# Layer 0's node table made beside the fetch of the edge rows, with ScalarE normalising

## The chip, the cores and the metric

One NeuronCore of a Trainium2 chip runs the whole program in one launch. The engines are PE (TensorE, matmuls and transposes), DVE (VectorE), ACT (ScalarE), POOL (GpSimd) and SP (SyncE, which only issues DMAs here). The metric is the device time of one execution in microseconds (us); lower is better.

## The reference, cut to what matters

Four layers of a graph network run over 6250 nodes of 128 features and 100,000 edges, sorted by destination. Each layer normalises the features, and layer 0 then gathers them over the edges:

```python
h = jnp.maximum(_layernorm(x, axis=-1), 0.0)
x = x + _L0_gnn_ref(h, edge_index, edge_weight, W, gamma, beta, 6250, 6250)

rows, cols = (A_indices[0], A_indices[1])        # src, dst
gathered = x[cols] * A_values[:, None]
h = jax.ops.segment_sum(gathered, rows, num_segments=m)
h = jnp.einsum('md,od->mo', h, W)
h = (h - mean) * jax.lax.rsqrt(var + BN_EPS) * gamma + beta
return jax.nn.relu(h)
```

So layer 0 takes its rows by `dst` (in sorted order) and adds them up by `src` (in random order). Layers 1 to 3 gather by `src` and add up by `dst`; layer 3 uses the small weights `Wl1` and `Wl2`.

## The kernel before

**Nodes and items.** The nodes lie in SBUF as `X`, 50 blocks of 128 rows (NBT is 50, the last block is empty, NB is 49). The edges are cut into rows of 128. Since the edges are sorted by destination, a row of edges touches one block of nodes or a few; each pair of an edge row and a block is an *item*, and there are 832 of them (ITEMS), in turns of 16 (RING). META is 896, seven chunks (CHUNKS) of 128 items.

**Prologue (lines 404 to 423, 591 to 713, 766 to 792, 1065 to 1083, 1270 to 1395).** SP loads `dst`, `X` and then the weights, in this order, on one queue. ACT issues the DMAs that copy `src`, `dst` and the edge weights to `e_meta` (three rows of 128 for an edge row, semaphore `small_copied`), and the block number of each edge to `blk_f` and `blk_i` (`blocks_out`), which only a sorting branch for unsorted inputs reads; that branch is not taken here. DVE and ACT count the edges below each block (lines 1282 and 1078), DVE turns the counts into the plan of the items (lines 1293 to 1327, `blocks_ready`): for each item its edge row and its block. POOL waits for `blocks_out` and `small_copied`, then fetches the edge rows of all items with seven indirect gathers (L703, semaphore `meta_rows`), fetches the rows once more in plain order (L708, L710), and sets two of the four sum buffers in DRAM to zero; the other two it did at the start (L636). PE transposes the three weights of layers 0 and 1 (L775), and DVE copies them out (L1362) and splits the biases into three bfloat16 parts (L1363 to L1368, `bias_split`). When the edge rows are in, DVE converts them to floats (L1377 to L1383), and 28 transposes on PE with 28 copies on DVE (L784, L1389) make `src_it`, `rel_it`, `w_it` and `m_row`, in which a column is an item. Last, 14 transposes and four copies make `blk_row` and `row_row` (L787 to L789, L1393, L1394), the lists from which the engines load the block and the edge row of an item into registers. A barrier (`barrier`, lines 263 to 267: all five engines drain and wait for each other) ends the prologue.

**Layer 0's table (`node_tables(0)`).** SP first stores `m_row` to DRAM (L543). DVE takes the statistics of the 50 blocks (L1400) and makes from them the reciprocal of the deviation and the product of that and minus the mean (L1423 to L1432), with a square root on ACT between (L1088). Then 13 batches of four blocks (the last of two) go through a pipeline: DVE multiplies and adds in two passes (L1406, L1410), PE transposes four blocks (L804), ACT copies them out with Relu (L1095), PE multiplies them with W0 (L820), ACT copies the product into the table `Tz` in SBUF (L1105). POOL and SP wait at the barrier that ends the table. `big`, the large region of SBUF, holds both the fetched edge rows (from 0 on) and `Tz` (from 0 on), so one follows the other.

**Layer 0's edges (`edges0`).** First DVE makes `to_spare` (L1521, L1522). Then all engines run through the items in steps; step n works on item n in its first stage and on earlier ones in the later stages. For an item: DVE builds a one-hot matrix (L1528), PE transposes it (L880), ACT copies it out (L1137), PE multiplies it with one block of `Tz` (L888), ACT scales by the edge weight (L1144). SP has meanwhile spread the 128 source ids of the item over all partitions (L448); DVE compares them with each other (L1536), PE adds up edges of the same source (L896), and six steps after the item's first stage DVE copies the result to `z_out` (L1544). L1550 and L1555 find repeated sources, whose rows are sent to a spare place. Every eighth step DVE makes eight columns of indices at once (L1568, semaphore `idx_ready`), and POOL adds each item's 128 rows into one of four buffers in DRAM with an indirect DMA (L727), in the order of the items; it waits for `idx_ready` at each eighth item, for `out_ready`, and for the previous scatter into the same buffer. SP also copies pieces of the edge attributes in this stage (L456), three DMAs for each turn of 16 items.

**After it.** `batch_norm` adds the four buffers and normalises; then come layers 1 to 3. At the start of each of these POOL sets the accumulator in `big` to zero (L747) while DVE begins `node_tables`. In layer 1 DVE first scales `Wl1` and `Wl2` (L1419 to L1421).

The order of the work is written out by hand; there is no planner. The main wait of the edge stage on POOL reads:

```python
if k % GROUP == 0:
    held(pool, ph["idx_ready"], uses[0])
held(pool, ph["out_ready"], i + 1)
held(pool, scattered[k % COPIES], uses[1])
```

## Time and profile before

| | |
|---|---|
| median of 3 runs | 5306.88 us (5306.61 to 5311.04) |
| the profiled execution | 5307.79 us |
| its span, first to last instruction | 5306.1 us |
| busy: PE, DVE, ACT, POOL | 4042.5, 3448.4, 1884.1, 3745.5 us |
| mean granted TensorE clock | 0.775 of full |

All times in the profile are from the start of the span. A busy share of the whole span says little here, since the stages have different limits; the stages are read from the windows and the timeline. "Idle before" is the time in which an engine did nothing ahead of an instruction, and the name behind "<-" is the releaser, the event that ended it. "issue" means that nothing in the profile was waited for. A name with q behind it (SPq, DVEq) is an engine's sequencer.

### The profile page before, as it was taken

What the parts mean: (1) busy time and instruction counts of PE and PEld (TensorE: products, weight loads), DVE (VectorE), ACT (ScalarE), POOL (GpSimd) and SP (SyncE); (2) the same over time, 40 slices, a digit from 0 to 9 for tenths busy, and PEclk for the clock granted to TensorE, in tenths of its full rate; (3) what the DMA queues carried; (4) which work ended last, traced back from release to release, by engine and by line L of the source; (5) the groups of instructions that cost most, each with busy time, mean ns of one, the idle gap of its engine ahead of it and who ended that gap; (6) DMA issues with size and microseconds to landing.
All of it is one profiled execution on the core that took longest, in us unless ns stands there. A gap on an engine that the chain in (4) does not pass through costs nothing. (4 is left out here: it accounts for less than half of the span.)

```text
span 5306.1 us, 109574 instructions
## 1 busy us (share of the span) xinstructions
PE 4042.5 (76%) x21313; PEld 3091.3 (58%) x21314; DVE 3448.4 (65%) x11120; ACT 1884.1 (36%) x5384; POOL 3745.5 (71%) x3284
## 2 busy tenths in 40 slices
PE   2888888888884466666666899998998678787787
PEld 2666666665663344444445677777776555565556
DVE  6655655656553633333335788888887688888886
ACT  3322222222221122222222433443343555555553
POOL 1888888888885377777773477777776277777772
PEclk8655555555555678888888999999999888888889
DMA  5656666665666266666663566666665233332332
GB/s 174 103 90 92 90 92 90 92 90 89 93 89 124 65 180 177 180 180 180 179 180 101 158 198 198 196 201 194 198 198 164 79 57 56 56 56 56 56 56 58
DMA packets 937554, 658.88 MB, mean 124 GB/s; under 512 B 402828, under 2 KB 878955, under 8 KB 934290
## 3 DMA queue, kind: packets, MB, share of 16 engines
q0 software_dynamic: 212176, 281.46, 26.3%
q1 hardware_dynamic: 722294, 372.22, 26.2%
q10 hardware_dynamic: 2812, 2.00, 0.2%
q8 instruction: 118, 1.93, 0.2%
q14 instruction: 154, 1.26, 0.1%
HBM read 462.32 MB, written 224.57 MB: 129 GB/s over the span
## 5 line engine op out<-in xcount | busy, mean ns | idle before, releaser
L727 POOL DMA_INDIRECT sums<-work,idx x832 | 1285.5, 1545 | 323.3 <-issue 173.9
L1497 DVE TENSOR_TENSOR x_and_big<-psum,x_and_big 128x129 f32 (+2 forms) x2496 | 830.3, 333 | 701.0 <-PE psum L843 484.8
L759 POOL DMA_INDIRECT G<-table,src_it x832 | 863.3, 1038 | 324.2 <-issue 252.9
L759 POOL DMA_INDIRECT G<-table,work x782 | 770.0, 985 | 269.5 <-issue 235.3
L759 POOL DMA_INDIRECT x_and_big<-table,work x782 | 762.0, 974 | 272.2 <-issue 236.2
L896 PE MATMUL psum<-work 128*128 128x128 f32 x1664 | 622.7, 476 | 194.5 <-DVE work L1544 167.2
L1144 ACT ACTIVATE work<-psum,work 128x128 f32<-128x128 f32 x832 | 306.1, 368 | 1067.0 <-PE psum L888 1065.2
L896 PEld LDWEIGHTS psum<-work 128*128 128x128 f32 x1664 | 408.2, 304 | 383.8 <-DVE work L1544 379.6
L990 PE MATMUL psum<-x_and_big,oh 128*128 x1664 | 513.3, 463 | 127.2 <-DVE x_and_big L1684 114.6
L843 PE MATMUL psum<-x_and_big,oh 128*128 x1664 | 322.4, 353 | 369.7 <-DMA x_and_big<-table,work 277.8
L888 PE MATMUL psum<-x_and_big,work 128*128 x1664 | 585.0, 454 | 0.0
L843 PEld LDWEIGHTS psum<-x_and_big,oh 128*128 128x128 f32 x1664 | 273.0, 248 | 462.8 <-issue 462.8
L1536 DVE TENSOR_SCALAR work<-G,src_it 128x128 f32<-128x128 int32 x832 | 270.8, 325 | 387.4 <-PE psum L896 380.4
L990 PEld LDWEIGHTS psum<-x_and_big,oh 128*128 128x128 f32 x1664 | 364.0, 229 | 215.1 <-issue 159.3
L880 PE MATMUL psum<-ident,oh 128*128 128x128 f32 x832 | 362.9, 436 | 88.3 <-issue 30.4
L888 PEld LDWEIGHTS psum<-x_and_big,work 128*128 128x128 f32 x1664 | 409.0, 305 | 34.3 <-issue 9.1
L1167 ACT ACTIVATE work<-work 128x512 f32<-128x512 f32 x208 | 131.2, 631 | 658.7 <-DVE work L1598 658.7
L1544 DVE COPY work<-psum 128x128 f32<-128x128 f32 x832 | 242.8, 292 | 184.5 <-DMA sums<-work,idx 181.1
L925 PE MATMUL psum<-x_and_big 128*128 x2496 | 345.1, 282 | 19.3 <-DVE work L1598 19.3
L1618 DVE TENSOR_TENSOR work<-work,G 128x1024 f32<-128x1024 f32 x208 | 254.7, 1224 | 142.4 <-DMA G<-table,src_it 141.2
L1484 DVE TENSOR_TENSOR oh<-iota,rel_it 128x512 f32<-128x512 f32 x416 | 285.2, 686 | 86.4 <-issue 82.1
L1194 ACT ACTIVATE x_and_big<-work 128x64 f32<-128x64 f32 x784 | 208.6, 336 | 365.8 <-DVE work L1663 365.8
(240 smaller groups left out, 7290.2 us busy)
## 6 DMA issues: line engine op xcount, KB each, us to landing
work<-e_pre SPq DMA_DIRECT2D x832, 128.0 KB
e_pre<-work SPq DMA_DIRECT2D x196, 512.0 KB
G<-e_meta SPq DMA_DIRECT2D x832, 64.0 KB, 3.1
work<-e_a SPq DMA_DIRECT2D x195, 128.0 KB
e_a<-in_edge_attr_dram SPq DMA_DIRECT2D x51, 488.0 KB
sums<-work,idx POOLq DMA_INDIRECT x832
G<-table,src_it POOLq DMA_INDIRECT x832
sums<-x_and_big POOLq DMA_DIRECT2D x4, 3264.0 KB
```

The lines of the kernel that those rows point to most:

```text
L727: pool.indirect_dma_start(sums[k % COPIES], bass.IndirectOffsetOnAxis(ap=idx[:, k:k + 1], axis=0), z_out[:, k, :], None, compute_op=ALU.ad ...
L759: pool.indirect_dma_start(to, None, tab, bass.IndirectOffsetOnAxis(ap=of[:, n:n + 1], axis=0)).then_inc(quad_in[n // 4 % AHEAD], 16)
L843: mm = t.matmul(bank[2 * o + j // 2][:, j % 2 * wid:(j % 2 + 1) * wid], oh[:, (k - 1) % 4 * 4 + j, :], at(G1, slot), start=True, stop=True)
L880: t.transpose(bank[s % 2][:, 0:P], oh[:, s, :], ident[:]).then_inc(ph["t_done"], 1)
L888: t.matmul(bank[2 + s % 2][:, 0:P], ohT[:, s % 4, :], at(Tz, b), start=True, stop=True).then_inc(ph["row_done"], 1)
L896: t.matmul(bank[4 + s % 2][:, 0:P], same[:, s % 4, :], scaled[:, s % 4, :], start=True, stop=True).then_inc(ph["sum_done"], 1)
L925: mm = t.matmul(pre_bank(half)[:, j % 2 * 256:j % 2 * 256 + 256], ohT2[:, (k - 1) % 2, j, :], Qp[:, bass.ds(b, 1), piece * 256:(piece + 1) ...
L990: mm = t.matmul(bank[4 + k % 2 * 2 + j // 2][:, j % 2 * 256:j % 2 * 256 + 256], oh[:, k % 4 * 4 + j, :], at(msg3, slot), start=True, stop= ...
L1144: a.activation(scaled[:, s % 4, :], bank[2 + s % 2][:, 0:P], ACT.Copy, scale=w_it[:, bass.ds(n - 4, 1)]).then_inc(ph["w_done"], 1)
L1484: v.tensor_tensor(oh[:, k % 4 * 4:k % 4 * 4 + 4, :], iota[:].unsqueeze(1).broadcast_to([P, 4, P]), rel_it[:, bass.ds(q * 4, 4)].unsqueeze( ...
L1497: v.tensor_tensor(to, ps, to, ALU.add).then_inc(EDGE[layer]["acc_done"], 1)
L1536: v.tensor_scalar(same[:, s % 4, :], src_b[:, s, :], src_it[:, bass.ds(n - 1, 1)], None, ALU.is_equal).then_inc(ph["same_ready"], 1)
```

## The change

What it does, by engine:

- **Memory.** The fetched edge rows and the setup region move behind the first NBT * 128 columns of `big`, so that `Tz` can be written while they are in use.
- **POOL.** Its gathers no longer wait for `blocks_out`. The barrier ahead of layer 0's table and the one behind it become one. The first turn of 16 scatters is written out; it waits for `idx_ready` at items 0, 2, 4, 6 and 8, the loop at each eighth as before.
- **PE.** The 14 transposes for `blk_row` and `row_row` come first, then the weights. Layer 0's table is made in the prologue: in step i PE transposes batch i, multiplies batch i - 1 and transposes two of the 28 pieces of the edge rows.
- **ACT.** After the counts it takes the square root, then normalises each block with one `Relu` with scale and bias from columns, four for a batch, and copies the transposed batch out. The product is now copied into `Tz` by DVE.
- **DVE.** Statistics and `layer_norm` come right behind the plan, with the copies of `blk_row` and `row_row` between the variance and the reciprocal; then the weights and biases, the conversions in another order with a signal after each, and a loop with two copies of edge pieces and one of the table in each step; then `to_spare`, then the barrier.
- **DVE, edge stage.** At steps 3, 5, 7 and 9 two columns of indices are made; from step 17 on eight at once, as before.
- **SP.** `X` gets a semaphore of its own. The first 16 loads of source ids and the store of `m_row` come ahead of the barrier, the attribute copies behind it.
- **Wl1 and Wl2** are scaled in `batch_norm`, behind the last sum and ahead of the wait for the mean, and no more in layer 1.

```diff
-        m_row = big[:, 8 * META:9 * META].bitcast(I32)
+        MB = NBT * 128
+        m_row = big[:, MB + 8 * META:MB + 9 * META].bitcast(I32)
...
-        setup_at = [16000]
+        setup_at = [MB + 9 * META + (NBT + 1) // 3 * P]
...
-            sp.dma_start(X[:, 0:NB - 1, :], x[0:(NB - 1) * P, :].rearrange("(b p) d -> p b d", p=P)).then_inc(weights_in, 16)
-            sp.dma_start(X[0:N - (NB - 1) * P, NB - 1, :], x[(NB - 1) * P:N, :]).then_inc(weights_in, 16)
+            sp.dma_start(X[:, 0:NB - 1, :], x[0:(NB - 1) * P, :].rearrange("(b p) d -> p b d", p=P)).then_inc(x_in, 16)
+            sp.dma_start(X[0:N - (NB - 1) * P, NB - 1, :], x[(NB - 1) * P:N, :]).then_inc(x_in, 16)
...
-            barrier(sp)
...
+                sp.wait_ge(starts_ready, 2)
+                sp.wait_ge(meta_rows, 16 * (CHUNKS + 2))
                 top(0)
                 for k in range(RING):
                     load(k, 0)
+                sp.wait_ge(meta_out, 4 * CHUNKS)
+                sp.dma_start(row_cols, m_row).then_inc(kept, 16)
+                barrier(sp)
+                half = sp.value_load(copy_to[0:1, 0:1], min_val=0, max_val=EPAD)
                 copy(0, FIRST)
...
-                else:
-                    sp.dma_start(row_cols, m_row).then_inc(kept, 16)
-                    sp.wait_ge(kept, 16)
-                    barrier(sp)
                 if layer == 0:
                     load_attributes(layer)
+                    sp.wait_ge(kept, 16)
...
-            pool.wait_ge(blocks_out, 32)
...
             for k in range(2, COPIES):
                 zero(k)
             barrier(pool)
-
-
             for k in range(COPIES):
                 pool.wait_ge(scattered[k], 16)
-            barrier(pool)
             ph = EDGE[0]
...
-                if k % GROUP == 0:
+                if k % GROUP == 0 or (isinstance(i, int) and i in (2, 4, 6)):
...
-            with pool.Fori(0, ITEMS // RING) as turn:
+            for k in range(RING):
+                scatter(0, k, k, (k // 2 + 1 if k < GROUP else 5, 16 * (k // COPIES + 1)))
+            with pool.Fori(1, ITEMS // RING) as turn:
                 for k in range(RING):
                     scatter(turn, k, turn * RING + k,
-                            (turn * 2 + k // GROUP + 1, turn * (16 * RING // COPIES) + 16 * (k // COPIES + 1)))
+                            (turn * 2 + k // GROUP + 4, turn * (16 * RING // COPIES) + 16 * (k // COPIES + 1)))
...
+            pe.wait_ge(blocks_ready, 2)
+            for c in range(CHUNKS):
+                at_cols = slice(c % 4 * P, (c % 4 + 1) * P)
+                t.transpose(bank[c // 4][0:1, at_cols], it_b[:, c:c + 1], ident[:])
+                mm = t.transpose(bank[2 + c // 4][0:1, at_cols], it_a[:, c:c + 1], ident[:])
+            mm.then_inc(meta_T, 1)
...
+            m_f = big[:, MB + 3 * META:MB + 7 * META]
+            count = len(batches(0))
+            pe.wait_ge(starts_ready, 3)
+            for i, b, n in batches(0) + [(count, 0, 0)]:
+                if i < count:
+                    pe.wait_ge(pre["xn_ready"], i + 1)
+                    if i >= 2:
+                        pe.wait_ge(pre["tT_ready"], i - 1)
+                    for j in range(n):
+                        mm = t.transpose(bank[i % 2][:, j * P:(j + 1) * P], xn[:, i % 2, j, :], ident[:])
+                    mm.then_inc(pre["t_done"], 1)
+                if i >= 1:
+                    o, m = (i - 1) % 2, batches(0)[i - 1][2]
+                    pe.wait_ge(pre["tT_ready"], i)
+                    if i >= 3:
+                        pe.wait_ge(pre["evac"], i - 2)
+                    for j in range(m):
+                        mm = t.matmul(bank[2 + o][:, j * P:(j + 1) * P], hT[:, o, j * P:(j + 1) * P], W0T[:], start=True, stop=True)
+                    mm.then_inc(pre["mm_done"], 1)
+                for q in (2 * i, 2 * i + 1):
+                    if q % CHUNKS == 0:
+                        pe.wait_ge(meta_rel, q // CHUNKS + 1)
+                    if q >= 4:
+                        pe.wait_ge(meta_out, q - 3)
+                    t.transpose(bank[4 + q % 4][:, 0:P], m_f[:, q * P:(q + 1) * P], ident[:]).then_inc(meta_T, 1)
             barrier(pe)
...
-            act.dma_start(bin_next, s_f[0:64, 5:6]).then_inc(bins_out, 16)
-            act.wait_ge(bins_out, 16)
+            act.dma_start(bin_next, s_f[0:64, 5:6]).then_inc(sort_bin, 16)
+
+            act.wait_ge(pre["ln_ready"], 1)
+            a.activation(ln[:, RSTD, :], ln[:, VAR, :], ACT.Sqrt).then_inc(pre["rstd_ready"], 1)
+            act.wait_ge(pre["ln_ready"], 2)
+            count = len(batches(0))
+            for i, b, n in batches(0) + [(count, 0, 0)]:
+                if i < count:
+                    if i >= 2:
+                        act.wait_ge(pre["t_done"], i - 1)
+                    for j in range(n):
+                        last = a.activation(xn[:, i % 2, j, :], X[:, b + j, :], ACT.Relu, scale=ln[:, RSTD, b + j:b + j + 1],
+                                            bias=ln[:, NMR, b + j:b + j + 1])
+                    last.then_inc(pre["xn_ready"], 1)
+                if i >= 1:
+                    o, m = (i - 1) % 2, batches(0)[i - 1][2]
+                    act.wait_ge(pre["t_done"], i)
+                    if i >= 3:
+                        act.wait_ge(pre["mm_done"], i - 2)
+                    a.activation(hT[:, o, 0:m * P], bank[o][:, 0:m * P], ACT.Copy).then_inc(pre["tT_ready"], 1)
+            act.wait_ge(sort_bin, 16)
             barrier(act)
...
-            for q in range(4 * CHUNKS):
-                dve.wait_ge(meta_T, q + 2)
-                to = (src_it, rel_it, w_it, m_row)[q // CHUNKS]
-                c = q % CHUNKS
-                v.tensor_copy(to[:, c * P:(c + 1) * P], bank[1 + q % 6][:, 0:P]).then_inc(meta_out, 1)
...
-                if layer == 0:
-                    link(stats(0, NBT))
...
-                if layer == 1:
-                    dve.wait_ge(wl_in, 16 * len(wl_loads))
-                    v.tensor_scalar(Wl1[:], Wl1[:], float(MUL ** -0.5), None, ALU.mult)
-                    link(v.tensor_scalar(Wl2[:], Wl2[:], float(0.25 * (2 * MUL) ** -0.5), None, ALU.mult))
-                    v.tensor_scalar(Wl2[32:64, 1, 0:32], Wl2[32:64, 1, 0:32], float(3 ** -0.5), None, ALU.mult)
...
+                between()
                 dve.wait_ge(pre["rstd_ready"], layer + 1)
...
+            def item_rows():
+                dve.wait_ge(meta_T, 1)
+                for half, (lo, hi) in enumerate(((0, 4), (4, CHUNKS))):
+                    n = (hi - lo) * P
+                    v.tensor_copy(blk_row[0:1, LEAD + lo * P:LEAD + lo * P + n], bank[0 + half][0:1, 0:n])
+                    last = v.tensor_copy(row_row[0:1, LEAD + lo * P:LEAD + lo * P + n], bank[2 + half][0:1, 0:n])
+                last.then_inc(starts_ready, 1)
+
+            dve.wait_ge(x_in, 32)
+            link(stats(0, NBT))
+            layer_norm(0, item_rows)
+            dve.wait_ge(weights_in, 16 * N_LOADS)
+            dve.wait_ge(meta_T, 2)
+            for k, w in enumerate((W0T, WmT, WuT)):
+                last = v.tensor_copy(w[:], bank[7][:, k * P:(k + 1) * P])
+            last.then_inc(starts_ready, 1)
...
+            dve.wait_ge(meta_rows, 16 * (CHUNKS + 2))
+            v.tensor_copy(chunked(m_f[:, 0:META]), m_i[:, :, 0, :]).then_inc(meta_rel, 1)
+            for c in range(CHUNKS):
+                lo = META + c * P
+                last = v.tensor_scalar(m_f[:, lo:lo + P], m_i[:, c, 1, :], it_off[:, c:c + 1], None, ALU.subtract)
+            last.then_inc(meta_rel, 1)
+            v.tensor_copy(chunked(m_f[:, 2 * META:3 * META]), m_w[:, :, 2, :]).then_inc(meta_rel, 1)
+            v.tensor_copy(m_f[:, 3 * META:4 * META], m_r).then_inc(meta_rel, 1)
+            dve.sem_inc(pre["scaled_ready"], len(batches(0)))
+            dve.wait_ge(blocks_out, 32)
+            for i in range(len(batches(0)) + 2):
+                for q in (2 * i, 2 * i + 1):
+                    if q < 4 * CHUNKS:
+                        dve.wait_ge(meta_T, q + 3)
+                        to = (src_it, rel_it, w_it, m_row)[q // CHUNKS]
+                        c = q % CHUNKS
+                        v.tensor_copy(to[:, c * P:(c + 1) * P], bank[4 + q % 4][:, 0:P]).then_inc(meta_out, 1)
+                if i >= 2:
+                    _, b, m = batches(0)[i - 2]
+                    dve.wait_ge(pre["mm_done"], i - 1)
+                    v.tensor_copy(flat3(Tz[:, b:b + m, :]), bank[2 + i % 2][:, 0:m * P]).then_inc(pre["evac"], 1)
+            dve.wait_ge(meta_out, CHUNKS)
+            link(v.tensor_scalar(to_spare[:], src_it[:], -1.0, iota_p[:, 0:1], ALU.mult, ALU.add))
+            link(v.tensor_scalar(to_spare[:], to_spare[:], float(NBT * P), None, ALU.add))
+            barrier(dve)
...
+                layer_norm(layer, lambda: None)
...
-                link(v.tensor_scalar(to_spare[:], src_it[:], -1.0, iota_p[:, 0:1], ALU.mult, ALU.add))
-                link(v.tensor_scalar(to_spare[:], to_spare[:], float(NBT * P), None, ALU.add))
...
-                    if k % GROUP == 1 and (not isinstance(n, int) or 1 < n <= ITEMS + 1):
+                    if isinstance(n, int) and n in (3, 5, 7, 9):
+
+                        dve.wait_ge(ph["spare_done"], n - 1)
+                        v.tensor_tensor(idx[:, n - 3:n - 1], spare[:, n - 3:n - 1], src_it[:, n - 3:n - 1], ALU.add).then_inc(ph["idx_ready"], 1)
+                    elif k % GROUP == 1 and (not isinstance(n, int) or 1 < n <= ITEMS + 1):
...
+                dve.wait_ge(wl_in, 16 * len(wl_loads))
+                v.tensor_scalar(Wl1[:], Wl1[:], float(MUL ** -0.5), None, ALU.mult)
+                link(v.tensor_scalar(Wl2[:], Wl2[:], float(0.25 * (2 * MUL) ** -0.5), None, ALU.mult))
+                v.tensor_scalar(Wl2[32:64, 1, 0:32], Wl2[32:64, 1, 0:32], float(3 ** -0.5), None, ALU.mult)
...
             for layer in range(4):
-                node_tables(layer)
+                if layer:
+                    node_tables(layer)
```

## Rows read from the trace of the kernel before

**Rows 1.** Windows, whole core: us, busy time (x instructions) per engine, clock, DMA share, GB/s

```profile
56.00:85.70 29.70, 8.20 (x45) 6.70 (x45) 17.09 (x52) 0.00 (x0) 10.03 (x11) 0.98 0.88 287
...
85.70:121.70 36.00, 20.21 (x150) 18.65 (x150) 28.39 (x84) 15.44 (x28) 0.00 (x0) 0.73 0.03 13
...
137.90:1677.00 1539.10, 1240.26 (x4121) 934.39 (x4119) 909.94 (x5039) 446.52 (x1647) 1285.49 (x832) 0.53 0.60 90
...
2896.00:4170.00 1274.00, 1127.34 (x8284) 909.81 (x8284) 1024.51 (x2099) 515.57 (x998) 868.69 (x833) 0.97 0.61 183
```

**Rows 2.** Groups of lines, 150 to 1670 us: busy us, mean ns | idle before, releasers

```profile
L727 POOL DMA_INDIRECT sums<-work,idx x823 | 1271.4, 1545 | 251.1 <-issue 172.4 <-DMA sums<-work,idx 59.5 <-DVE work L1544 19.2
```

**Rows 3.** Timeline, POOL, first scatter: start us, us, what [idle before <-releaser]

```profile
137.92 1.70 POOL L727 DMA_INDIRECT sums<-work,idx  x1 [69.78 <-DVE work L1544]
```

**Rows 4.** Timeline, 44 to 72 us; last, SP's DMA queue from 0 to 44 us

```profile
44.91 0.20 DVE L1326 TENSOR_REDUCE s_f<-x_and_big 64x1 f32<-64x50 f32 x1
...
54.94 1.04 POOL L703 DMA_INDIRECT x_and_big<-e_meta,x_and_big  x1 [41.65 <-DMA blk_f<-x_and_big]
...
57.83 0.90 PE L775 MATMUL psum<-ident,x_and_big 128*128 128x128 f32 x3 [19.33 <-DMA work<-in_L_gnn_beta_dram]
...
62.61 1.21 DVE L1368 TENSOR_TENSOR x_and_big<-x_and_big 1x1024 bf16<-1x1024 f32 x1
...
63.00 1.65 POOL L703 DMA_INDIRECT x_and_big<-e_meta,x_and_big  x1 [0.30 <-issue]
...
69.67 0.17 DVE L1377 TENSOR_SCALAR x_and_big<-x_and_big 128x7 f32<-128x7 f32 x1 [5.85 <-DMA x_and_big<-e_meta]
...
q1 hardware_dynamic: 2508, 3.87, 34.6%
```

**Rows 5.** Timeline, 73 to 100 us

```profile
73.94 5.60 PE L784 MATMUL psum<-ident,x_and_big 128*128 128x128 f32 x28 [15.21 <-DVEq L1384]
...
82.13 0.68 DVE L1393 CAST blk_row<-psum 1x512 int32<-1x512 f32 x1 [1.78 <-PE psum L789]
...
85.89 9.77 DVE L1400 BATCH_NORM_STATS2 bn_raw<-x_and_big 128x6 f32<-128x128 f32 x50 [1.56 <-POOLq L266]
...
96.92 1.28 ACT L1088 ACT_TABLE_LOAD   x1 [63.18 <-DVE ln L1429]
...
99.35 0.69 DVE L1406 TENSOR_TENSOR work<-x_and_big,ln 128x512 f32<-128x512 f32 x1
```

**Rows 6.** ACT: timeline at 4112 us (eight of L1214), then groups of 0 to 290 us

```profile
4112.63 2.47 ACT L1214 ACTIVATE work<-x_and_big,rdeg 128x128 f32<-128x128 f32 x8 [12.89 <-DVE rdeg L1695]
...
L1144 ACT ACTIVATE work<-psum,work 128x128 f32<-128x128 f32 x95 | 34.9, 368 | 109.2 <-PE psum L888 107.4 <-issue 1.8
...
L1137 ACT ACTIVATE work<-psum 128x128 f32<-128x128 f32 x98 | 26.3, 270 | 6.6 <-PE psum L880 6.0 <-issue 0.2
...
L1095 ACT ACTIVATE work<-psum 128x512 f32<-128x512 f32 x12 | 7.2, 598 | 8.9 <-PE psum L804 8.9
```

**Rows 7.** Timeline of DVE, first steps of layer 0's edge stage

```profile
123.14 0.48 DVE L1528 TENSOR_SCALAR oh<-iota,rel_it 128x128 f32<-128x128 f32 x2
...
126.70 0.29 DVE L1536 TENSOR_SCALAR work<-G,src_it 128x128 f32<-128x128 int32 x1 [3.08 <-DMA G<-e_meta]
...
132.09 0.28 DVE L1544 COPY work<-psum 128x128 f32<-128x128 f32 x1
...
136.55 0.17 DVE L1568 TENSOR_TENSOR idx<-spare,src_it 128x8 int32<-128x8 f32 x1
...
147.25 0.17 DVE L1568 TENSOR_TENSOR idx<-spare,src_it 128x8 int32<-128x8 f32 x1 [0.24 <-DMA sums<-work,idx]
```

**Rows 8.** Timeline of DVE: batch norm, start of layer 1, start of layer 2

```profile
1742.01 0.69 DVE L1753 TENSOR_REDUCE work<-psum 128x128 f32<-128x512 f32 x1 [5.97 <-PE psum L1050]
...
1793.19 5.44 DVE L1420 TENSOR_SCALAR Wl<-Wl 128x256 f32<-128x256 f32 x1
...
2897.20 4.85 DVE L1426 TENSOR_SCALAR ln<-ln 128x50 f32<-128x50 f32 x1
```

94 lines of the change are left out of this document (35 added, 59 removed).

## The prediction

> **What bounds the kernel now.** I read the stage windows first [rows 1], then the group that fills the long stage [rows 2], then the order of events ahead of it [rows 3 to 5]. The windows show a stage of 1539.1 us, from 137.9 to 1677, that holds all 832 indirect scatters of POOL [rows 1]: 1539.1 / 832 = 1.850 us each. The group's line gives the same from inside: a scatter is 1.545 us, and of the 251.1 us of idle time before 823 of them 172.4 us is issue, 0.3 us each, and only 19.2 us is put down to DVE [rows 2]. So once it runs, layer 0's edge stage goes at POOL's pace, whatever PE (1240.3 us busy there) and DVE (909.9 us) do; what stands ahead of the first scatter moves its end one for one. POOL sat idle for 69.78 us before that scatter, which starts at 137.92 [rows 3]. I therefore sum one thing: when the first scatter starts. Ahead of it stand, in a row, the fetch of the edge rows and their transposes (to 84), the table of layer 0 (85.7 to 121.7, with the DMAs at 3% and POOL at nothing [rows 1]), and 16.2 us in which the edge pipeline fills.
>
> **Part 1: the rows are fetched earlier.** The item plan is done on DVE at 45.1 (L1326) [rows 4]. Before, POOL began the seven gathers at 54.94, after 41.65 us put down to the landing of blk_f [rows 4]. That wait goes; what is late next is the plan itself, so I start the gathers at 46.2 (1.1 us for POOL's register load and branch, an estimate). From the first gather to the conversion that waits for them took 69.67 - 54.94 = 14.7 us [rows 4]; new landing 60.9.
>
> **Part 2: statistics and normalising go beside that.** X must be in. Its 3.2 MB and the 0.4 MB of dst are first on SP's queue, and by 44 us that queue had moved 3.87 MB [rows 4], so I take no wait; had it landed only with the weights behind it (57.83), this chain would be 11 us later. DVE then goes, from 46.0: 50 statistics 9.77 to 55.8; to the variance 1.26 (95.66 to 96.92) to 57.0; there the four row copies now stand, about 0.6 each by their first, 0.68, so 2.3, to 59.3, which cover ACT's table load and square root (1.5 us); reciprocal and NMR 0.8, to 60.1 [rows 5]. ACT may start then. DVE itself goes on with the three weight copies and the bias split. They took 63.82 - 58.73 = 5.1 us after the weights' transposes [rows 4], and the weights, in at 57.83, are ready by then even if the gathers beside them delay them 1 us. So 65.2. The offsets and the source ids, 1.3 us of the 4.27 us that all conversions took (69.67 to 73.94) [rows 4, 5], give PE its first edge rows at 66.5; the rest ends at 69.5. The rows (60.9) have 4.3 us of slack against DVE at 65.2.
>
> **Part 3: the table by ACT.** Before, DVE did two passes of 0.69 per batch of four blocks (L1406) [rows 5], 1.4 us a batch. Now ACT does four Relu of 128x128 with scale and bias both read from columns. The trace has none with two. The nearest has one: eight in 2.47 us, about 0.295 apart with their overlap; a column costs about 0.368 - 0.270 = 0.10 more than a constant [rows 6]. So a Relu is between 0.295 (the second column free) and 0.39; I take 0.39, since the first column was not free either: 1.58 a batch. The transposed copy is 0.598 less 0.11 overlap, 0.49 [rows 6]. ACT pays 2.07 a batch. PE's table loads took 18.65 us for 12.5 batches [rows 1], 1.5 each, and two of the 28 edge transposes, 0.2 each at the most (28 in 5.60 [rows 5]), ride on each: 1.9, just below. DVE pays two copies of 0.2 and one evacuation of about 0.6. So ACT sets the pace. PE waits for the source ids with batch 1 not yet transposed, so ACT has only three batches and one copy behind it when PE comes back; its second copy starts at 67.6. Left are 12 copies (5.9 us) and 9.5 batches (15.0 us), and I add 1.5 us of handoffs: 90.0. The last product and evacuation take 1.2 us, to_spare on DVE 1.4 (from the barrier at 121.7 to the first one-hot at 123.14 [rows 7]): the barrier opens at 92.7; before it was 121.7. The 28 edge transposes and their copies are inside that.
>
> SP is moved too: its first 16 source rows now follow the rows' landing and the bias stores, at about 69. DVE took a step each 1.4 us at most (11 steps from 132.37 to 147.42 [rows 7]) and they kept ahead of it, so they need at most 22 us and are out before the barrier. DVE waited 3.08 us for the first of them [rows 7]; that goes. Its attribute copies now come before the second 16 rows, but SP has 11 items of time there. POOL's last two zeroings follow the gathers, 9 us earlier than before; all that the DMAs moved then was through by 85.7, when their share fell to 3%, so these are in before 92.7. The one barrier that goes stood beside these; I count it in the stretch replaced.
>
> **Part 4: pairs.** Before, eight indices were made at once, at 136.55, though the first product was copied at 132.09 to 132.37; the scatter started 1.2 us after the indices [rows 3, 7]. With pairs the first two indices come at step 3, ahead of that copy. From the first one-hot (123.14) to the copy's end (132.37) are 9.23 us, less 3.08 of wait, plus two pair instructions with their waits (0.5): 6.7. So the first scatter starts at 92.8 + 6.7 + 1.2 = 100.7; I take 101. The next risk is item 8, whose indices still come at step 17: 147.42 was 15.05 us after that first copy [rows 7], so 116 now, and item 8 is due at 101 + 8 x 1.85 = 115.8. I count 0.3 us of stall, up to 2 where PE is slow.
>
> **Part 5: the Wl scalings.** They move to a place where DVE sat idle for 5.97 us waiting for the mean (L1753) [rows 8]; if that cover were gone they would cost under 1 us. At layer 1 they took 5.44 us beside a long POOL memset [rows 8]. It would be wrong to book that as a gain: the tensor_scalar on the variance, a 128x50 one, took 4.85 us in layer 2 beside the same memset [rows 8], and it will be the one that waits in layer 1. Only what stood behind the memset in the queue gets ahead of it: about 1 us. The Trainium skill, "SBUF — State Buffer", gives the rule in its section "Who interferes with whom": a DVE tensor_scalar in a 2-port mode and a GpSimd instruction exclude each other for a whole instruction. The trace agrees; without rule and row one would forecast 4.5 us more, 5265.
>
> **Sum.** 137.92 - 101 = 36.9, less 0.3, plus 1 = 37.6. The profiled execution took 5307.79 us, 1.7 around its span of 5306.1, and 0.9 above the median: 5307.8 - 37.6 = 5270.2. I say 5270.
>
> **Rivals.** *The gathers are late.* POOL makes descriptors while DVE is busy, where before DVE was idle for most of it. For: the first gather took 1.04 us with DVE idle, the last, beside the bias split, 1.65 [rows 4]. Against: bn_stats makes most of the company. Price: 7 x 0.6 = 4.2 us, just the slack, and if the landing stays late by 5 more, 5275. The same page of the Trainium skill says, in its section "SBUF: two separate sides", that a DVE copy in a 2-port mode keeps GpSimd from writing descriptors; whether statistics do, no run here shows.
>
> *Slow PE in the table.* The clock was 0.98 of full (2.4 GHz) from 56 to 85.7 and averaged 0.73 over the old table stage, where PE began after a pause [rows 1]. At 1.2 GHz throughout, PE's 1.9 us a batch would be 3.8 if all of it had been measured at full clock; part of it was not, and I take 3.3: 13 x (3.3 - 2.07) = 16 us more, 5286. Against: PE has work from 58 on.
>
> *Slower than before: the clock of layer 2.* PE is busy for 1127 of 1274 us there at a mean of 0.97 [rows 1]. If an earlier start shifts what the chip grants, a mean under 0.94 gives the 37.6 us back (1127 x (0.97 / 0.94 - 1) = 36); at 0.91 it costs 74 us and the kernel takes about 5344. For: PE is the busiest engine there. Against: nothing in that stage is changed, and the three runs lie within 4.4 us.
>
> *The gain does not arrive,* since something other than the first scatter (SP's attribute pieces, say) holds the end of the edge stage: 5306. Against: POOL waits 0.3 us and then issues, 1539 us long.
>
> **Chances.** Forecast 0.72, with its own range 5261 to 5279: ACT's Relu at 0.295 ends the table 4 us earlier, half of the handoffs away 1, the stall at item 8 or 2 us of weights later. Late gathers 0.11, slow PE 0.11, layer 2's clock 0.02, no gain 0.04. The range, 5259 to 5283, leaves out those last cases and the worst of the slow PE. A measurement can tell about 0.2% (10.6 us) from no change: faster 0.95, same 0.03, slower 0.02.
>
> **What would show it.** POOL's first scatter at 101 (97 to 107); still 1.85 us per scatter to the end; the first gather at 46; ACT 2.0 to 2.2 us per batch and no wait of DVE for meta rows; layer 1's variance instruction at about 4.5 us. Wrong would be: scatters apart by more than 1.86, a hole after the eighth, X landing after 46, or the table paced by PE.

## The result, and the profile after

| | before | changed |
|---|---|---|
| median on the same chip (7 runs each) | 5309.23 us (5302.67 to 5311.04) | 5289.85 us (5284.59 to 5295.75) |
| ratio | | 0.9966 [0.9956, 0.9975] |
| profiled execution, span | 5307.79, 5306.1 us | 5284.59, 5282.9 us |
| first one-hot of the edge stage | 123.14 | 108.99 |
| first scatter, last scatter | 137.92, 1675.39 | 116.19, 1655.63 |
| POOL's memset at the start of layer 1, 2 | 1792.95, 2896.57 | 1773.25, 2876.68 |

The change is faster by 0.34% (19.4 us on the medians), about half of the 37.6 us forecast, and the time lies above the range. The milestones say where to look. The first scatter comes 21.7 us earlier, not 36.9. Of this 2.0 us are lost between first and last scatter, so layer 2 starts 19.9 us earlier. Of the 23.2 us by which the profiled span is shorter, the last 3.3 are layers 2 and 3, in which nothing was changed; over the kernels below layer 2 alone, from POOL's memset at its start to that of layer 3, took 1268.3 to 1278.6 us. So totals of one execution scatter by more than most edits here are worth, and the experiments are read at milestones of the prologue.

The windows of the changed kernel that answer to [rows 1], with the same columns:

```profile
56.00:85.70 29.70, 12.86 (x73) 11.46 (x74) 23.14 (x79) 15.08 (x37) 3.04 (x5) 0.62 0.79 262
85.70:108.90 23.20, 14.09 (x111) 12.18 (x109) 11.33 (x30) 11.88 (x28) 0.00 (x0) 1.00 0.21 63
116.20:1657.20 1541.00, 1240.11 (x4140) 941.39 (x4138) 910.44 (x5065) 448.51 (x1655) 1286.19 (x832) 0.53 0.60 89
2876.00:4147.90 1271.90, 1131.10 (x8284) 911.34 (x8284) 1024.10 (x2099) 515.75 (x998) 867.23 (x833) 0.97 0.61 183
```

The edge stage is POOL's as before: 1541.0 us with 1286.2 busy, and layer 2 has its clock of 0.97. In the first two windows no engine is full (the columns are those of [rows 1]: PE, its weight loads, DVE, ACT, POOL, clock, DMA share, GB/s). DVE is at 23.1 of 29.7 us and then at 11.3 of 23.2, ACT at 11.9 of 23.2: the table is paced by a chain of handoffs, not by an engine. The group that answers to [rows 2] (130 to 1650 us) and POOL's timeline, to [rows 3]:

```profile
L723 POOL DMA_INDIRECT sums<-work,idx x821 | 1269.0, 1546 | 251.7 <-issue 181.2 <-DMA sums<-work,idx 52.5 <-DVE work L1593 18.0
```

```profile
116.19 1.70 POOL L723 DMA_INDIRECT sums<-work,idx  x1 [56.86 <-DVE work L1593]
...
129.27 1.54 POOL L723 DMA_INDIRECT sums<-work,idx  x1 [0.30 <-issue]
132.04 1.54 POOL L723 DMA_INDIRECT sums<-work,idx  x1 [1.22 <-DVE work L1593]
```

The last line of the second fence is item 8 with its stall: 1.22 us of idle time where 0.30 is usual. The timeline from 44 to 76 us, which answers to [rows 4, 5]:

```profile
44.68 0.20 DVE L1362 TENSOR_REDUCE s_f<-x_and_big 64x1 f32<-64x50 f32 x1
...
45.52 1.28 ACT L1100 ACT_TABLE_LOAD   x1 [12.23 <-DVEq L1363]
...
47.23 1.04 POOL L702 DMA_INDIRECT x_and_big<-e_meta,x_and_big  x1 [34.17 <-issue]
...
52.64 9.76 DVE L1398 BATCH_NORM_STATS2 bn_raw<-x_and_big 128x6 f32<-128x128 f32 x50 [7.76 <-DMA x_and_big<-in_x_dram]
...
54.89 0.95 POOL L702 DMA_INDIRECT x_and_big<-e_meta,x_and_big  x1 [0.30 <-issue]
...
60.11 0.90 PE L779 MATMUL psum<-ident,x_and_big 128*128 128x128 f32 x3 [11.97 <-DMA work<-in_L_gnn_beta_dram]
...
66.41 3.19 ACT L1108 ACTIVATE work<-x_and_big,ln 128x128 f32<-128x128 f32 x8 [2.55 <-DVEq L1416]
...
71.52 1.09 DVE L1449 CAST x_and_big<-x_and_big 128x896 f32<-128x896 int32 x1
...
72.66 0.69 PE L806 MATMUL psum<-ident,x_and_big 128*128 128x128 f32 x2 [3.37 <-DVE x_and_big L1449]
```

The gathers start at 47.2 and each takes 0.95 to 1.04 us. The rows are there when DVE comes to them: the cast at L1449 waits for no DMA. But the statistics start at 52.64, after 7.76 us of waiting for `X`, where 46.0 was forecast. Everything behind is late by about that: the first Relu 66.41 (forecast 60.1), the first edge pieces 72.66 (66.5). A step of the table, once it runs (97.5 to 101 us):

```profile
97.13 0.60 ACT L1116 ACTIVATE work<-psum 128x512 f32<-128x512 f32 x1 [0.38 <-PE psum L791]
...
97.81 1.13 PE L799 MATMUL psum<-W0T,work 128*128 128x128 f32 x8 [0.72 <-ACT work L1116]
98.78 0.38 PE L806 MATMUL psum<-ident,x_and_big 128*128 128x128 f32 x2
...
99.09 0.29 DVE L1464 COPY work<-psum 128x128 f32<-128x128 f32 x1 [1.42 <-PE psum L806]
...
99.49 0.68 DVE L1468 COPY x_and_big<-psum 128x512 f32<-128x512 f32 x1
...
100.32 0.91 PE L799 MATMUL psum<-W0T,work 128*128 128x128 f32 x6 [0.72 <-ACT work L1116]
```

The period is 100.32 - 97.81 = 2.51 us, not 2.07, with DVE idle for 1.42 of it and ACT for 0.38 (up to 97.13). The order of starts shows a ring: the product (L799), then PE's two edge transposes (L806), then DVE's two copies of them (L1464), then the evacuation of the product before (L1468, 99.49 to 100.17), then the next product at 100.32. The profile names ACT as the product's releaser, but ACT's copy of that step began at 97.13; the evacuation ends 0.15 us before the product starts, and only it fits.

### The profile page after: what moved, and what is told of

The parts are those of the page before. It is cut to its first block and busy times, and to the rows that moved or that the text cites. A ratio compares the mean times of both kernels' runs of the same rounds, so it can differ in the third digit from the quotient of the medians.

```text
span 5282.9 us, 109578 instructions
## 1 busy us (share of the span) xinstructions
PE 4043.0 (77%) x21313; PEld 3101.9 (59%) x21314; DVE 3433.2 (65%) x11110; ACT 1897.1 (36%) x5421; POOL 3743.4 (71%) x3284
## 3 DMA queue, kind: packets, MB, share of 16 engines
q0 software_dynamic: 212176, 281.46, 26.4%
## 5 line engine op out<-in xcount | busy, mean ns | idle before, releaser
L723 POOL DMA_INDIRECT sums<-work,idx x832 | 1286.2, 1546 | 311.6 <-issue 183.4
L858 PEld LDWEIGHTS psum<-x_and_big,oh 128*128 128x128 f32 x1664 | 288.9, 262 | 457.2 <-issue 457.1
L1005 PEld LDWEIGHTS psum<-x_and_big,oh 128*128 128x128 f32 x1664 | 359.5, 227 | 214.1 <-issue 159.1
L1536 DVE TENSOR_TENSOR oh<-iota,rel_it 128x512 f32<-128x512 f32 x416 | 284.4, 684 | 82.6 <-issue 79.7
```

The lines of the kernel that those rows point to most:

```text
L723: pool.indirect_dma_start(sums[k % COPIES], bass.IndirectOffsetOnAxis(ap=idx[:, k:k + 1], axis=0), z_out[:, k, :], None, compute_op=ALU.ad ...
L858: mm = t.matmul(bank[2 * o + j // 2][:, j % 2 * wid:(j % 2 + 1) * wid], oh[:, (k - 1) % 4 * 4 + j, :], at(G1, slot), start=True, stop=True)
L1005: mm = t.matmul(bank[4 + k % 2 * 2 + j // 2][:, j % 2 * 256:j % 2 * 256 + 256], oh[:, k % 4 * 4 + j, :], at(msg3, slot), start=True, stop= ...
L1536: v.tensor_tensor(oh[:, k % 4 * 4:k % 4 * 4 + 4, :], iota[:].unsqueeze(1).broadcast_to([P, 4, P]), rel_it[:, bass.ds(q * 4, 4)].unsqueeze( ...
```

## The experiments

Each kernel is the changed one with the edit shown. Times are milestones in us of one profiled execution; *Relu* is ACT's first normalising instruction, *layer 2* POOL's memset at its start. e1 to e7 were executed once each, so their totals say little; e8 to e11 were executed five times.

| | statistics | Relu | one-hot | scatter, first | last | layer 2 | time |
|---|---|---|---|---|---|---|---|
| changed | 52.64 | 66.41 | 108.99 | 116.19 | 1655.63 | 2876.68 | 5284.59 |
| e1 | 46.78 | 60.84 | 103.41 | 110.61 | 1649.40 | 2870.52 | 5287.36 |
| e2 | 54.45 | 68.21 | 101.94 | 109.06 | 1647.94 | 2869.94 | 5286.17 |
| e3 | 52.89 | 66.66 | 107.70 | 114.90 | 1655.08 | 2873.89 | 5285.08 |
| e4 | 55.75 | 69.51 | 112.07 | 123.44 | 1661.79 | 2883.02 | 5297.31 |
| e5 | 54.00 | 67.76 | 110.34 | 117.54 | 1655.17 | 2874.14 | 5282.90 |
| e6 | 53.69 | | 104.24 | 111.44 | 1651.98 | 2869.74 | 5277.74 |
| e7 | 52.17 | 65.93 | 105.07 | 112.27 | 1651.61 | 2871.77 | 5281.21 |
| e8 | 46.02 | 60.09 | 96.10 | 103.37 | 1641.13 | 2864.20 | 5278.75 |
| e9 | 45.94 | 60.02 | 93.34 | 101.16 | 1640.09 | 2857.92 | 5273.44 |
| e10 | 45.93 | | 93.80 | 101.06 | 1640.35 | 2860.26 | 5276.53 |
| e11 | 46.23 | 60.31 | 91.36 | 99.29 | 1637.52 | 2860.05 | 5267.98 |

**e1: why is X late?** All four zeroings of `sums` follow the edge rows.

```diff
-            for k in range(2):
-                zero(k)
             pool.wait_ge(tails_in, 6 * 16)
...
-            for k in range(2, COPIES):
+            for k in range(COPIES):
                 zero(k)
```

> All four sum buffers are set to zero behind the gathers; none at the start. Theory A (X lands late because the two early zeroings share the DMA engines with it): X in by 35 to 45, the statistics start at 45.2 right behind the plan instead of 52.64, ACT's first Relu at 59 instead of 66.4, the first scatter about 6 us earlier, at 110 (109 to 112). Theory B (the load is slow by its own queue, whatever runs beside it): the statistics start at 52 +- 1 and the first scatter stays at 116. Either way the zeroings must be in by the barrier at 101 to 107: they start at 58 and move 13 MB, 32 us at the 410 GB/s the windows show.

The timeline of e1:

```profile
46.78 9.76 DVE L1396 BATCH_NORM_STATS2 bn_raw<-x_and_big 128x6 f32<-128x128 f32 x50 [1.35 <-issue]
```

The wait for X is gone (1.35 us of issue is left), and the Relu and the one-hot come 5.6 us earlier. In the six kernels that keep two early zeroings (e2 to e7) the statistics start between 52.2 and 55.8. So those zeroings, 3.3 MB each, issued at 11.5 us, are what holds X.

**e2: what paces the table?** DVE evacuates before it copies the edge pieces.

```diff
+                if i >= 2:
+                    _, b, m = batches(0)[i - 2]
+                    dve.wait_ge(pre["mm_done"], i - 1)
+                    v.tensor_copy(flat3(Tz[:, b:b + m, :]), bank[2 + i % 2][:, 0:m * P]).then_inc(pre["evac"], 1)
                 for q in (2 * i, 2 * i + 1):
...
-                if i >= 2:
-                    _, b, m = batches(0)[i - 2]
...
```

> In each step of the table loop DVE copies the table's batch out before the two edge pieces. Theory A (the loop of 2.51 us is product, two edge transposes, two DVE copies, then the evacuation that the next product waits for): the step falls to 2.1 to 2.2 us, ACT's four Relu and copy without a pause; first scatter 4 to 6 us earlier, 111 to 112. Theory B (PE waits for ACT's copy of the transposes, as the trace names it, 0.72 us a step): the step stays at 2.5 and the first scatter at 116.

A step of e2:

```profile
87.85 1.65 ACT L1108 ACTIVATE work<-x_and_big,ln 128x128 f32<-128x128 f32 x4
...
89.31 0.49 DVE L1468 COPY work<-psum 128x128 f32<-128x128 f32 x2 [0.93 <-PE psum L806]
89.39 0.59 ACT L1116 ACTIVATE work<-psum 128x512 f32<-128x512 f32 x1
...
89.72 0.68 DVE L1462 COPY x_and_big<-psum 128x512 f32<-128x512 f32 x1
89.87 1.65 ACT L1108 ACTIVATE work<-x_and_big,ln 128x128 f32<-128x128 f32 x4
```

The period is 2.02 us and ACT has no idle time: now ACT does set the pace, as forecast. From Relu to one-hot 33.73 us against 42.58. e1, e4 and e5 have the table of the changed kernel, and there this stretch took 42.57, 42.56 and 42.58 us, so the 8.85 us are the order's and not an accident of the execution. The theory that PE waits for ACT's copy is refuted.

**e3: the clock.** 14 matmuls of 512 columns, whose results nobody reads, before the weights' transposes and six after them.

```diff
+            for _ in range(14):
+                t.matmul(bank[6][:, :], ones[:], repeat(ident[:], 4), start=True, stop=True)
             pe.wait_ge(weights_in, 16 * N_LOADS)
...
+            for _ in range(6):
+                t.matmul(bank[6][:, :], ones[:], repeat(ident[:], 4), start=True, stop=True)
             pe.wait_ge(starts_ready, 3)
```

> 20 matmuls of 128x512 that nobody reads are added on PE ahead of the table, 14 before the weights' transposes and 6 behind them, so that PE is busy from 48 to about 66. Theory A (the table's first steps are slow because the clock was granted at half while PE sat idle): clock 1.00 from 68 on, the steps before 80 take 2.5 instead of 3.0 us, first scatter about 1.5 to 2 us earlier, 114 to 115. Theory B (the clock is low there whatever PE does): clock 0.5 to 80, first scatter 116, or later if the filler delays the weights.

Two windows of the changed kernel, then the same two of e3, then a product of e3:

```profile
66.00:70.00 4.00, 1.09 (x4) 0.72 (x4) 3.65 (x10) 3.59 (x10) 0.00 (x0) 0.50 1.02 420
...
74.00:78.00 4.00, 4.00 (x20) 4.00 (x20) 2.40 (x6) 2.91 (x7) 0.00 (x0) 0.50 0.96 305
```

```profile
66.00:70.00 4.00, 1.18 (x6) 0.42 (x4) 3.65 (x10) 3.34 (x9) 0.00 (x0) 1.00 1.02 418
...
74.00:78.00 4.00, 4.00 (x31) 4.00 (x29) 2.91 (x10) 3.40 (x9) 0.00 (x0) 0.78 0.98 271
```

```profile
78.97 1.13 PE L803 MATMUL psum<-W0T,work 128*128 128x128 f32 x8 [0.72 <-DVE x_and_big L1472]
```

PE ran the first steps at the lower level (0.50, 1.2 GHz) in the changed kernel, at 3.0 us a step; with work ahead of them it did so for only part of that time (the clock still fell, against the expectation of 1.00 from 68 on). From Relu to one-hot 41.04 against 42.58: the slow start cost 1.5 us. At full clock the steps are still 2.51 apart. Here the profile names the true releaser, the evacuation.

The record of the clock has to be held against the instructions. First the changed kernel, two groups of instructions in the slow start and one after it; then e2, the same two, and its window from 74 to 78:

```profile
73.14 1.06 PE L791 MATMUL psum<-ident,work 128*128 128x128 f32 x4
...
73.99 1.92 PE L799 MATMUL psum<-W0T,work 128*128 128x128 f32 x8
...
80.25 1.13 PE L799 MATMUL psum<-W0T,work 128*128 128x128 f32 x8 [0.72 <-ACT work L1116]
```

```profile
74.94 1.06 PE L791 MATMUL psum<-ident,work 128*128 128x128 f32 x4
75.80 1.92 PE L799 MATMUL psum<-W0T,work 128*128 128x128 f32 x8
...
74.00:78.00 4.00, 3.54 (x17) 3.54 (x18) 3.74 (x13) 1.96 (x5) 0.00 (x0) 1.00 1.03 355
```

e2's record says 1.00, and yet eight products take 1.92 us as in the changed kernel at 0.50, and not the 1.13 of full clock. The same holds for e4 and e7. So the slow start was in all these executions, with or without a trace of it in the record, and e2 gained nothing by the clock.

**e4: the pairs alone.** The first indices in eights again.

```diff
-                    if isinstance(n, int) and n in (3, 5, 7, 9):
+                    if False:
...
-                if k % GROUP == 0 or (isinstance(i, int) and i in (2, 4, 6)):
+                if k % GROUP == 0:
```

> Undoes the pairs alone: eight indices at once at step 9, as before. Theory A (the pairs move the first scatter from step 9 to step 6, but the indices of items 8 to 15 then come late): first scatter 4 to 5 us later, at 120.5, and no hole of 0.9 us after the eighth scatter, so the last scatter is only 3 to 4 us later than with pairs, at 1659. Theory B (the scatter waits for the first product, not the indices): first scatter unchanged at 116.

One-hot to first scatter takes 11.37 us, with pairs 7.20: 4.17 gained. There is no hole at item 8, so at the last scatter (one-hot to last 1549.72 against 1546.64) 3.1 are left, give or take the 1 us by which this stretch scatters.

**e5: pairs for items 8 to 13 too,** into a buffer of their own, with a wait on POOL for each pair; 14 and 15 still come at step 17. The diff shows DVE's part.

```diff
+                    elif isinstance(n, int) and n in (11, 13, 15):
+                        dve.wait_ge(ph["spare_done"], n - 1)
+                        v.tensor_tensor(idx2[:, n - 11:n - 9], spare[:, n - 3:n - 1], src_it[:, n - 3:n - 1], ALU.add).then_inc(ph["idx_ready"], 1)
```

> The indices of items 8 to 13 are made in pairs too (steps 11, 13, 15), in a tile of their own. Theory A (item 8 waits for its indices until step 17, which is the hole of 0.9 to 1.9 us): no hole, first scatter 7.2 us after the first one-hot as with the changed kernel, and first to last scatter 1538 us instead of 1539.4. Theory B (the hole is a late product of item 8, or a late source row from SP): the hole stays.

The eighth and ninth scatter of e5, at the place of the hole:

```profile
130.62 1.57 POOL L723 DMA_INDIRECT sums<-work,idx  x1 [0.30 <-DVE work L1593]
132.50 1.54 POOL L723 DMA_INDIRECT sums<-work,idx  x1 [0.30 <-DMA sums<-work,idx]
```

No hole: item 8 waited for its indices, and that cost 0.9 us (1.22 - 0.30). First to last scatter took 1537.63 us against 1539.44 (before: 1537.47), but this scatters as much: 1537.6 to 1539.3 over the five kernels with the longer pairs, 1538.8 to 1540.5 over the six without, about 1.2 apart on average.

**e6: who should normalise?** DVE again in two passes, ACT evacuates; the rest of the change stays.

```diff
+                    v.tensor_tensor(to_xn, X[:, b:b + m, :], ln[:, RSTD, b:b + m].unsqueeze(2).broadcast_to([P, m, D]),
+                                    ALU.mult).then_inc(pre["scaled_ready"], 1)
+                    dve.wait_ge(pre["scaled_ready"], i + 1)
+                    v.tensor_tensor(to_xn, to_xn, ln[:, NMR, b:b + m].unsqueeze(2).broadcast_to([P, m, D]),
+                                    ALU.add).then_inc(pre["xn_ready"], 1)
...
-                        last = a.activation(xn[:, i % 2, j, :], X[:, b + j, :], ACT.Relu, scale=ln[:, RSTD, b + j:b + j + 1],
+                    a.activation(flat3(Tz[:, b:b + m, :]), bank[2 + o][:, 0:m * P], ACT.Copy).then_inc(pre["evac"], 1)
```

> DVE normalises in the new place (two passes of 0.69 us a batch, behind its conversions), and ACT copies the transposes out with Relu and the product into the table, as before. Theory A (moving the normalising to ACT bought nothing by itself, since it put the copy of the product on DVE, behind the edge pieces): DVE pays about 1.9 us a step, and from the start of the statistics to the first one-hot it is 51 to 52 us instead of 56.35. Theory B (ACT's share is what lets the table be hidden): DVE, starting 9 us later than ACT could, makes it 58 us or more.

From the statistics to the one-hot 50.55 us, against 56.35 with ACT normalising. Though DVE could only begin to normalise at 76.47, 22.8 us after the start of the statistics where ACT's first Relu came after 13.8, its steps of 1.78 us came in first. So as made, ACT's normalising bought nothing: it cost 5.8 us. But the cause is the order and not the engine: e2, with ACT normalising and the evacuation first, needs 47.49 us for this stretch, 3.1 less than e6.

**e7: the bias split** to the end of the edge stage, and SP's stores with it.

```diff
-            v.tensor_scalar(w2s[:], w2s[:], 0.5, None, ALU.mult)
-            link(v.tensor_scalar(br[:, BR_B2:BR_B2 + P], br[:, BR_B2:BR_B2 + P], 0.5, None, ALU.mult))
...
                 edge_steps(dve, 6, lambda turn: None, body)
+                v.tensor_scalar(w2s[:], w2s[:], 0.5, None, ALU.mult)
+                link(v.tensor_scalar(br[:, BR_B2:BR_B2 + P], br[:, BR_B2:BR_B2 + P], 0.5, None, ALU.mult))
...
                 barrier(dve)
```

> The scaling of w2s and the split of the biases (4.8 us of DVE ahead of the conversions) move to the end of layer 0's edge stage, where DVE waits for POOL, and SP stores the biases there. Theory A (PE's first edge pieces, and with them the whole table loop, wait for that split): from the start of the statistics to the first one-hot 51.5 to 52.5 us instead of 56.35. Theory B (the loop is bound by ACT from its start at 66): less than 1.5 us of change.

52.90 us from the statistics to the one-hot, 3.45 less, near theory A. PE's first product came 4.15 us after the Relu against 7.58, 3.4 earlier, and took 1.92 us as in the changed kernel, so the 3.45 are the split's: the first edge pieces, and the table loop with them, waited for it.

**e8: all of it.** e1, e2, e5, e7, and filler matmuls as in e3, with one after the transposes in place of six.

> Zeroings behind the gathers, the table's copy first in each step, six more items in pairs, the split at the end of the edge stage, and 15 filler matmuls on PE, on top of the change. If the four pieces found add up (6 us for X, 8.9 us for the loop with its tail, 4 to 5 us for the split, 1 us for the clock, 1 us for the hole): statistics at 46.8, first one-hot at 88 to 90, first scatter at 95 to 97, the last at 1633, and about 20 us less than the changed kernel: 5265 to 5272. If they share one wait, or the zeroings are not in by then, the first scatter is at 101 or later.

Median 5274.73 us (5269.17 to 5278.75, 5 runs), ratio 0.9943 [0.9929, 0.9956]. The table went as meant, but the one-hot came at 96.10. The drains at the barrier (duration in ns), and the one-hot in the timeline:

```profile
L266 POOLq DRAIN  x1: 37702/37702/37702, 58.4 to 58.4; - x1
...
L266 DVEq DRAIN  x1: 10/10/10, 89.8 to 89.8; - x1
L266 SPq DRAIN  x1: 124/124/124, 92.6 to 92.6; - x1
```

```profile
96.10 0.48 DVE L1573 TENSOR_SCALAR oh<-iota,rel_it 128x128 f32<-128x128 f32 x2 [6.39 <-POOLq L266]
```

The expectation, 88 to 90, is missed, as is its total of 5265 to 5272. DVE stood at the barrier from 89.8. POOL's drain came last, at 58.4 + 37.7 = 96.1: it waited behind four zeroings. With two it took 22.0 us in the changed kernel (57.7 to 79.7), hidden by the slow table. In e1 it took 37.2 too (to 96.3), hidden for the same reason.

**e9: one early zeroing** on e8.

```diff
+            zero(0)
             pool.wait_ge(tails_in, 6 * 16)
...
-            for k in range(COPIES):
+            for k in range(1, COPIES):
                 zero(k)
```

> Edit: e8_all with one of the four zeroings of sums issued early (before the plan) in place of none; the other three still follow the edge rows. Question: what opened e8_all's barrier at 96.0, 6.4 us after DVE was there? There POOL's drain behind four zeroings (13.1 MB) began at 58.4 and took 37.7 us, with the DMA engines at a share of 1.0 and about 410 GB/s; behind two it took 22.0 us in the changed kernel. Theory Z (the drain is held by the zeroings' bytes): three give about 29 to 30 us, so POOL is there at 88 to 89 and the barrier opens when DVE is, 3 us or less after e8_all's DVE (89.8), since one early zeroing delays X by no more than half of what two did (6 to 9 us): first one-hot at 90 to 94, first scatter at 97 to 101, 2 to 6 us before e8_all's 103.4. Theory S (SP is late: its sixteen source-row loads took 26.4 us to issue and its row_cols came at 91.0): the first one-hot stays at 95 to 97. Total 5270 to 5277, ratio about 0.993 to 0.995.

```profile
L266 POOLq DRAIN  x1: 28744/28744/28744, 57.9 to 57.9; - x1
...
L266 DVEq DRAIN  x1: 10/10/10, 89.7 to 89.7; - x1
L266 SPq DRAIN  x1: 123/123/123, 93.2 to 93.2; - x1
```

SP's issues of its source rows, durations in ns (least/median/most):

```profile
L443 SPq DMA_DIRECT2D G<-e_meta x16: 332/333/16367, 67.0 to 92.3; - x16
```

Both theories were right in turn. POOL's drain took 28.7 us as expected and was done at 86.6; then SP was last, at 93.2, since its sixteen source rows took 25.7 us to issue. Of these 16.4 are one single issue, from 67.0 on, while the DMA engines were at a share of 1.0; half of the sixteen took 0.333 us at most. X was not late at all (statistics at 45.94). Median 5275.94 us, ratio 0.9941 [0.9927, 0.9954].

**e10: e9 with e6's table,** DVE normalising and ACT evacuating (the diff of e6).

> Edit: e9_one_early, but normalising is back on DVE (two passes) and the evacuation on ACT, as in e6_dve_norm. Question: is the table's pace still the limit of the barrier once the other delays are gone, and which engine should normalise? Theory D (DVE's loop is the faster: e6_dve_norm took 1.83 us a step, e8_all 2.02): table shorter by 12 x 0.19 = 2.3 us, first one-hot 1 to 3 us before that of e9_one_early, unless POOL's drain (88 to 89) or SP holds it. Theory A (ACT's loop in e8_all's order is as good, since PE at full clock was what both waited for): within 1 us of e9_one_early. Total 5268 to 5277 in either case: stages behind scatter by 5 us from run to run, so the verdict goes by the first one-hot.

The one-hot stands at 93.80, but DVE itself was last here, with no wait at the barrier, where in e9 DVE was there at 89.7. The step was fast again (1.78 us), but DVE could start it only at 66.04, behind copies and conversions, where ACT had started at 60.02. So with the evacuation first ACT is the better engine, by 4 us, hidden in e9 by SP. About 1 us of the 4 is PE's slow start (products 2.56 and 1.97 us apart, later 1.78), which e9 had not. Median 5277.22 us, ratio 0.9940 [0.9926, 0.9953].

**e11: e9 with eight of the sixteen rows behind SP's barrier.**

```diff
-                for k in range(RING):
+                for k in range(RING // 2):
                     load(k, 0)
...
                 barrier(sp)
+                for k in range(RING // 2, RING):
+                    load(k, 0)
```

> Edit: e9_one_early, with SP loading eight of its first sixteen source rows ahead of the barrier and eight behind it. In e9_one_early DVE was at the barrier at 89.7 and POOL's drain done at 86.6, but SP came at 93.2: its sixteen loads took 25.69 us to issue beside the zeroings (in the changed kernel, where they came after the zeroings, 9.47). Theory S (those loads held e9's barrier): eight are out by 80 to 82, SP waits for the last transposes instead, and the barrier opens about 0.5 to 1.5 us after DVE is there (row_cols is issued behind the last transpose's copy, at 88.3, in 0.4): first one-hot at 89.8 to 91, first scatter at 97 to 98.5, against 93.3 and 101.2 in e9. Rival (the edge steps then wait for rows 8 to 15, or SP's barrier is late for another reason): the first one-hot is early but a hole shows at scatters 3 to 10, or the one-hot stays at 93. Total 5266 to 5276: 3 us is about the scatter of the later stages, so the verdict goes by the first one-hot and the first scatter.

```profile
91.36 0.48 DVE L1576 TENSOR_SCALAR oh<-iota,rel_it 128x128 f32<-128x128 f32 x2 [1.43 <-SPq L266]
```

The first scatter is at 99.29, no hole follows, and layer 1 starts 37.8 us earlier than before. One-hot and first scatter are 0.4 and 0.8 us behind what was expected: SP is still 1.4 us late. Its eight rows were out at 90.7 and not at 80 to 82, since the first of them alone took 16.2 us to issue. So it is mostly the zeroings that hold SP, and less the number of rows; no kernel with a fast table had its rows clear of the zeroings. Median 5267.98 us (5263.04 to 5275.19, 5 runs), before on the same chip 5302.23, ratio 0.9935 [0.9922, 0.9949]. This version beats both kernels. The ratios of e8 to e11 overlap, so their totals do not rank them.

## Why the prediction was wrong

The quantity to sum was right: POOL's pace of 1.85 us a scatter held to the end, and a first scatter earlier by 21.7 us moved layer 2 by 19.9. The first scatter was forecast at 101 and came at 116.19; the one-hot at 92.7 to 92.8 and came at 108.99, 16.2 us late. By its steps:

- **Part 1, the gathers:** right. First at 47.2 for 46.2 (the 1.1 us between plan and gather, for which no row stood, were 2.35), none slower than 1.04 us beside the statistics, and no wait of DVE for the rows. The rival of late gathers did not occur.
- **Part 2, "by 44 us that queue had moved 3.87 MB, so I take no wait":** failed, 6.6 us. The queue's total says what it moved, not which load was complete; this step rested on an average where a landing was needed. The two zeroings of POOL, on another queue, were not weighed. e1 shows them as the cause. The rest of the chain was right to 0.4 us: statistics to Relu 13.8 for 14.1.
- **Part 3, "so ACT sets the pace":** failed, and this is the largest step. The forecast summed the work of each engine and took the largest, 2.07 us. The prices were right: four Relus and a copy take 2.02 in e2 (a Relu of two columns 0.482 us with its overlap 0.39 apart, the upper bound taken). But DVE, with least to do, had its evacuation behind two copies that wait for PE's last work of the step, and PE's next product waits for the evacuation: a ring of 2.51, shown by e2, where only the order of two pieces on DVE changes. From Relu to one-hot 42.6 us for 32.7, of which e2 gets 8.85 back.
- **Slow PE:** the rival was priced at 16 us for the whole table. It held for the first steps only, and cost 1.5 (e3), before and beside the ring's 8.85. "PE has work from 58 on" was wrong: PE did 0.9 us of work between 56 and 66.
- **SP and the zeroings, "in before 92.7":** true for POOL in the changed kernel (its drain ended at 79.7). SP's source rows, put at about 69, were issued from 83.49 on, since the weight loads ahead of them took 24.1 us to issue beside the zeroings (54.87 to 78.96); the slow table hid that. e8 and e9 show what was not weighed: SP's row loads and POOL's drain both grow with the zeroings that run beside them, and each held the barrier once the table was fast.
- **Part 4, pairs:** one-hot to scatter 7.2 for 7.9, right. The stall at item 8 was counted at 0.3 of up to 2; it was 0.9. The mechanism was named, its size was off.
- **Part 5, Wl:** right that it is no gain of 4.5 us. The variance instruction waits now in layer 1, as forecast (4.5 expected, 4.89 measured), which answers to [rows 8]:

```profile
1773.25 5.48 POOL L745 MEMSET x_and_big<- 128x6450 f32 x1 [5.52 <-DVEq L266]
...
1773.88 4.89 DVE L1407 TENSOR_SCALAR ln<-ln 128x50 f32<-128x50 f32 x1
```

  From the memset's start to ACT's square root it was 7.23 us before and 5.86 after, 1.4 gained for 1; of layer 1 as a whole (memset to memset) 0.2 is seen (1103.62 to 1103.43), within its scatter of 1100.4 to 1105.1 over these kernels. The rule of the Trainium skill, "SBUF — State Buffer", section "Who interferes with whom", is borne out again: the tensor_scalar lasts as long as POOL's memset does.

Sum of the misses, from 37.6 down to 19.9: X 6.6, less 0.3 in the chain behind it; ring and clock 9.9, less 1.0 between one-hot and scatter, so 15.2 at the first scatter; 1.7 in the scatters (2.0 for 0.3, of which 0.9 is the hole and the rest within their scatter); 0.8 in layer 1 (0.2 for 1). That is 17.7.

e11 comes near the forecast, with the first scatter at 99.29 (forecast 101) and a profiled time of 5267.98 us (forecast 5270). That confirms less than it seems to. With X in time and the evacuation first e11 has what the forecast took for granted, but the longer pairs, the clock kept up and the split gone were not in the forecast: the split alone was worth 3.4 us. The nearness is in part luck.

## What to carry to other kernels

In a loop over several engines, draw the order of the waits before taking the busiest engine as the pace: an engine that is idle for more than half of a step can set the period when it does its urgent piece behind one that waits for somebody's last. Whether a load has landed is read from who waits for it, or not known; a queue's bytes do not say it, and big transfers on other queues can delay it, as e1 shows. And where one delay is taken away, ask each participant of the next barrier, SP and POOL's drain too, when it would be there: here SP and POOL came 3 and 6 us behind DVE as soon as DVE was fast.

## What the runs showed of the hardware

- With two zeroings of 3.3 MB each on POOL's queue beside SP's load of X (3.2 MB), DVE waited for X until 52.2 to 55.8 us in seven kernels; with one or none it did not wait (statistics at 45.9 to 46.8, behind the plan). When X landed in those is not seen, so neither is how the delay grows with the bytes.
- POOL's drain grows with the zeroings ahead of it: 37.2 and 37.7 us behind four, 28.6 to 29.2 behind three, 20.9 to 22.0 behind two. In e8 the DMA engines moved 402 GB/s on average at a share of 1.0 in that time.
- SP's issue of the same sixteen row loads took 9.5 us when the zeroings were over and 25.7 and 26.4 beside them (e9, e8). In e9 one issue took 16.4 us of it; in e8 the median was 1.1 and the longest 3.8.
- ACT's table load stood at 45.52, ahead of its 16.8 us wait for the variance, so it cost nothing; the forecast had it behind the wait, covered by the row copies.
- The recorded clock from 56 to 66 us was 0.50 in the changed kernel, e5 and e6 and 1.00 in e2, e4 and e7, with PE busy for 0.90 us in each; but in all six the table's first eight products took 1.91 or 1.92 us, where later ones took about 1.1. So the recorded clock alone does not tell here how fast PE runs; the duration of a known instruction does. Why the records differ stays open.
